# Expert router on DVE: tokens and routing weights transposed in 32 x 32 blocks, DMAs that exchange the blocks, logits in plain fp32 on four column quarters

## What is computed

```python
x = x + layernorm(attention(layernorm(x)))      # 16 heads of 16 channels, softmax over 1024 keys
x = x + layernorm(experts(layernorm(x)))

def experts(x):                                 # xf: 8192 tokens x 256
    logits = l2norm(xf) @ l2norm(gate_w).T      # 16 experts
    scores = sigmoid(logits)
    topk_scores, topk_idx = top_k(scores, 8)
    combine = one_hot(topk_idx) * (topk_scores / sum(topk_scores))      # summed over k: tokens x 16
    y = (silu(xf @ w_gate[e]) * (xf @ w_up[e])) @ w_down[e]             # for every expert e, hidden size 128
    routed = sum over e of y[e] * combine[:, e]
    shared = (silu(xf @ sw_gate) * (xf @ sw_up)) @ sw_down
    return routed + shared
```

## Time and profile before

| what | us |
|---|---|
| median of 3 runs (range) | 2789.33 (2788.68 to 2798.21) |
| profiled execution, its own time | 2794.4 |
| its span, first to last instruction | 2792.5 |
| TensorE matmul busy | 2700.3 (97%) |
| DVE busy | 2203.7 (79%) |
| ACT busy | 1628.2 (58%) |
| POOL busy | 1040.4 (37%) |

### The profile page before, as it was taken

The page is one execution under the profiler, slowest core; times in us unless marked ns, Lnnn a source line. Parts: engine busy times, 40 slices in busy tenths (PEclk is TensorE's granted clock), DMA queues, the critical chain, the costliest instruction groups (busy, mean ns, idle before and its releaser), DMA issues.

```text
span 2792.5 us, 49038 instructions
## 1 busy us (share of the span) xinstructions
PE 2700.3 (97%) x17634; PEld 1775.7 (64%) x17634; DVE 2203.7 (79%) x4585; ACT 1628.2 (58%) x3159; POOL 1040.4 (37%) x1057
## 2 busy tenths in 40 slices
PE   5999999999999999999998999999999999999997
PEld 3445445454454444544543488888888888888886
DVE  5799999989989999999899566666666666666654
ACT  1588888878878788788788733333333333333332
POOL 4042563644635636545358353111111111111112
PEclk8899999999999999999999999999999999999999
DMA  5102333122122222330232323222222222223222
GB/s 119 27 28 58 70 76 72 57 62 66 43 66 66 69 65 64 73 66 28 66 93 76 94 71 101 80 71 75 84 84 82 75 76 84 80 69 84 80 73 54
DMA packets 126595, 197.39 MB, mean 71 GB/s; under 512 B 12288, under 2 KB 74768, under 8 KB 124304
## 3 DMA queue, kind: packets, MB, share of 16 engines
q1 hardware_dynamic: 126352, 194.25, 26.8%
HBM read 108.74 MB, written 17.30 MB: 45 GB/s over the span
## 4 chain that ended last, share of the span: by engine, by line
PE 80%; DVE 13%; ACT 3%; issue 2%; POOL 1%; DMA 0%; POOLq 0%; SPq 0%; ACTq 0%; DVEq 0%
PE o_bank L597 14%; PE y_bank L775 14%; PE g_bank L761 13%; PE u_bank L761 13%; PE st_bank L568 10%; DVE score_max L1164 10%; PE sm_bank L587 8%; PE job_bank L587 2%; ACT probs L1056 2%; PE sm_bank L693 2%; PE job_bank L693 1%; DVE qk_parts L1187 1%; PE job_bank L716 1%; PE job_bank L729 0%; DVE row_max L1171 0%
## 5 line engine op out<-in xcount | busy, mean ns | idle before, releaser
L1056 ACT ACTIVATE probs<-st_bank 128x512 f32<-128x512 f32 x2023 | 1079.2, 603 | 268.9 <-PE st_bank L568 258.6
L1164 DVE TENSOR_REDUCE score_max<-sm_bank 128x1 f32<-128x512 f32 x1601 | 1023.3, 681 | 69.5 <-PE sm_bank L587 63.6
L568 PE MATMUL st_bank<-qk_stack 64*128 64x512 f32 x2023 | 743.4, 427 | 7.1 <-ACT probs L1056 6.9
L587 PE MATMUL sm_bank<-qk_stack 64*128 64x512 f32 x1601 | 655.8, 461 | 27.8 <-DVE score_max L1164 22.1
L597 PE MATMUL o_bank<-probs,v_quad 128*32 128x512 f32 x4096 | 552.7, 612 | 0.7 <-ACT probs L1056 0.7
L568 PEld LDWEIGHTS st_bank<-qk_stack 64*128 64x128 f32 x2023 | 350.2, 186 | 274.7 <-ACT probs L1056 232.6
L587 PEld LDWEIGHTS sm_bank<-qk_stack 64*128 64x128 f32 x1601 | 288.7, 189 | 296.8 <-DVE score_max L1164 268.3
L1312 DVE TENSOR_TENSOR h<-gate_act,u_bank 128x512 f32<-128x512 f32 x256 | 176.2, 688 | 310.9 <-ACT gate_act L1010 310.7
L1010 ACT ACTIVATE gate_act<-g_bank 128x512 f32<-128x512 f32 x272 | 162.4, 597 | 416.0 <-PE u_bank L761 415.9
L1021 ACT ACTIVATE h_hi<-h 128x512 fp32r<-128x512 f32 x272 | 172.1, 633 | 327.8 <-DVE h L1315 290.2
L1595 POOL TENSOR_SCALAR f_x_in<-f_x_in,f_mv,f_rstd 128x256 f32<-128x256 f32 x64 | 90.3, 1422 | 617.2 <-DVE f_rstd L1226 617.2
(11 more groups left out here) (248 smaller groups left out, 4854.6 us busy)
## 6 DMA issues: line engine op xcount, KB each, us to landing
cb<-comb_dram SPq DMA_DIRECT2D x256, 256.0 KB, 3.5
qk_stack<-qk_parts SPq DMA_DIRECT2D x180, 256.0 KB, 5.5
x_in<-in_x SPq DMA_DIRECT2D x8, 1024.0 KB, 5.5
o_part<-o_sb SPq DMA_DIRECT2D x64, 128.0 KB, 2.7
sum_part<-o_sb SPq DMA_DIRECT2D x64, 128.0 KB, 2.8
x_res<-in_x SPq DMA_DIRECT2D x16, 512.0 KB, 3.9
x<-x_res SPq DMA_DIRECT2D x16, 512.0 KB, 4.1
f_x_in<-x SPq DMA_DIRECT2D x16, 512.0 KB, 3.9
```

Of the source, the lines that this page charges most:

```text
L568: mm(bank_of(tile)[:, :], k_stack[q][p][rows, kc * CH:(kc + 1) * CH], q_stack[q][p][rows, f * HALF:(f + 1) * HALF], start=True, stop=True) ...
L587: mm(shared_bank[bank][:, :], q_stack[q][p][rows, tok:tok + CH], k_stack[q][p][rows, half * HALF:(half + 1) * HALF], start=True, stop=True ...
L1056: nc.scalar.activation(probs[kc % 2][:, HEAD_AT[j], :], bank_of(4 * U + j)[:, :], ACT.Exp).then_inc(exp_done, 1)
L1164: v.reduce_max(score_max[f][:, HC * (2 * p + e) + c, half:half + 1], shared_bank[max_bank[n]][:, :], AX_X).then_inc(smax_read, 1)
```

## The change

The transposes of the router leave TensorE. For the tokens, SP issues 16 DMAs (`swap`), from SBUF to SBUF, which exchange the 32 x 32 blocks between the partition quarters and the channel quarters of each 128 x 128 tile, in pieces of 32 floats; DVE then transposes within the blocks (`turn_x`, twice 128 x 512), back into `fx_in`, which now holds the transposed tokens in plain fp32. `xt_hi` and `xt_lo` read them there. The logits take them as moving operand in plain fp32: two steps k of four products, each with the gate weights (32 columns, of which 16 repeat the others) as stationary operand, 128 token columns, and its own quarter of the output partitions. DVE turns the logits (`turn_logits`) and the routing weights (`turn_comb`) too, and four DMAs store the latter. The order of the pieces changes: the layer norm's statistics begin in the group before (e = 14 to 16), the swap comes at e = 7 (`SWAP_AT`), `turn_x` at 7, `xt_hi` and `xt_lo` at 8 and 9, and the load of the tokens of g + 2 at e = 13. In group 0's router the swap stands ahead of the weight loads of experts 12 to 16.

```diff
+        def transposed_x(k):
+
+            return fx_in[:, :, :].rearrange("p (k c) d -> p k (c d)", k=KD)[:, k, :]
+
+
+        comb_flat = comb_dram.rearrange("e t -> (e t)")
+
+        def comb_row(g, e):
+            return comb_flat[(g * EXPERTS + e) * GROUP:(g * EXPERTS + e + 1) * GROUP]
...
             def store_comb(g):
-                wait_apart(sp, E["cbT_read"], g + 1, f_passed["sp"])
-                sp.dma_start(comb_dram[:, bass.ds(g * GROUP, GROUP)], combT[:, :]).then_inc(E["comb_stored"], 16)
+                wait_apart(sp, E["comb_turned"], g + 1, f_passed["sp"])
+                rows = comb_flat[g * EXPERTS * GROUP:(g + 1) * EXPERTS * GROUP].rearrange(
+                    "(p c a j) -> a p c j", p=BLOCK, c=HALVES, a=BLOCKS)
+                for a in range(BLOCKS):
+                    sp.dma_start(rows[a], combT[BLOCK * a:BLOCK * (a + 1), :].rearrange("p (c j) -> p c j", c=HALVES)
+                                 ).then_inc(E["comb_stored"], 16)
+
+            def swap(g):
+
+                wait_apart(sp, E["f_x_normed"], GC * (g + 1), f_passed["sp"])
+                if g == 0:
+                    sp.wait_ge(E["gT_ready"], KD)
+                    sp.wait_ge(E["sq_ready"], GC)
+                else:
+                    wait_apart(sp, E["xT_ready"], KD * g, f_passed["sp"])
+                rows = fx_in[:, :, :].rearrange("p c (k f) -> p (c k) f", k=KD)
+                for b in range(BLOCKS):
+                    for a in range(BLOCKS):
+                        sp.dma_start(swapped[BLOCK * a:BLOCK * (a + 1), :, BLOCK * b:BLOCK * (b + 1)],
+                                     rows[BLOCK * b:BLOCK * (b + 1), :, BLOCK * a:BLOCK * (a + 1)]
+                                     ).then_inc(E["x_swapped"], 16)
 
             def load_cb(g, e):
                 if e == 0:
-                    wait_apart(sp, E["comb_stored"], 16 * (g + 1), f_passed["sp"])
+                    wait_apart(sp, E["comb_stored"], 16 * BLOCKS * (g + 1), f_passed["sp"])
                     if g == 0:
                         sp.wait_ge(st_ready, 4 * UNITS * BATCHES)
                 n = EXPERTS * g + e
                 if not (isinstance(n, int) and n < 4):
                     wait_apart(sp, E["h_done"], n - 3, f_passed["sp"])
                 sp.dma_start(cb[e % 4][:, :],
-                             comb_dram[e, bass.ds(g * GROUP, GROUP)].partition_broadcast(128)).then_inc(cb_loaded[e % 4], 16)
...
                 gather(b, 5)
                 load_shift(b, 7)
                 if last:
+                    swap(0)
                     for e in range(EARLY, ALL_E):
                         load_w(e)
-                    sp.wait_ge(E["xT_ready"], KD)
-                    sp.wait_ge(E["sq_ready"], GC)
+                gather(b, 6)
+                if last:
+                    sp.wait_ge(E["xT_read"], KD)
+                    sp.wait_ge(E["lg_ready"], 1)
                     f_load_x(1)
...
+                    if e == SWAP_AT and not last:
+                        swap(g + 1)
+                    if e == 13 and g + 2 < GROUPS:
+                        wait_apart(sp, E["xT_read"], KD * (g + 2), f_passed["sp"])
+                        wait_apart(sp, E["lg_ready"], g + 2, f_passed["sp"])
+                        f_load_x(g + 2)
...
             def lg(g, par):
                 take_bank("LG", g, 0)
-                pe.wait_ge(E["xT_read"], KD * (g + 1))
+                pe.wait_ge(E["xT_ready"], KD * (g + 1))
                 if isinstance(g, int) and g == 0:
                     pe.wait_ge(E["gT_read"], KD)
...
+                for k in range(KD):
+                    tokens = transposed_x(k).rearrange("p (c a j) -> p a c j", a=BLOCKS, j=BLOCK)
+                    for a in range(BLOCKS):
+                        last = mm(job_bank[BLOCK * a:BLOCK * (a + 1), 0:CH], gT[:, k, :], tokens[:, a, :, :],
+                                  start=(k == 0), stop=(k == KD - 1), skip_group_check=True)
                 last.then_inc(E["lg_ready"], 1)
...
-                    if not last and e in (4, 5):
-                        xt(g + 1, 1 - par, e - 4)
                     if not last and e == 7:
                         lg(g + 1, 1 - par)
-                    if not last and e == 12:
-                        cbt(g + 1)
...
-                a_(fxT[par][0][:, k, :], job_bank[:, :], ACT.Identity).then_inc(E["xT_hi_ready"], 1)
+                a_(fxT[par][0][:, k, :], transposed_x(k), ACT.Identity).then_inc(E["xT_hi_ready"], 1)
...
+                to = x_sq[:, :] if g == 0 else job_bank[:, D:2 * D]
+                a_(to, fx_in[:, c, :], ACT.Square, accum_out=n2[:, c:c + 1]).then_inc(E["sq_ready"], 1)
...
+            def turn_x(g, k):
+                dve.wait_ge(E["x_swapped"], 16 * BLOCKS * BLOCKS * (g + 1))
+                dve.wait_ge(E["sq_ready"], GC * (g + 1))
+                blocks = swapped[:, :, :].rearrange("p (c k) f -> p k c f", k=KD)[:, k, :, :]
+                v.transpose(transposed_x(k).rearrange("p (c f) -> p c f", c=GC), blocks).then_inc(E["xT_ready"], 1)
+
             def xt_lo(g, par, k):
                 dve.wait_ge(E["xT_hi_ready"], KD * g + k + 1)
-                v.tensor_tensor(fxT[par][1][:, k, :], job_bank[:, :], fxT[par][0][:, k, :].bitcast(F32),
+                v.tensor_tensor(fxT[par][1][:, k, :], transposed_x(k), fxT[par][0][:, k, :].bitcast(F32),
                                 ALU.subtract).then_inc(E["xT_read"], 1)
 
-            def sum_logits(g):
-                dve.wait_ge(E["lg_small_read"], g + 1)
+            def turn_logits(g):
+                dve.wait_ge(E["lg_ready"], g + 1)
+                if g > 0:
+                    dve.wait_ge(E["route_chain"], ROUTE * g)
+                v.transpose(lg_turns[:, :, :].rearrange("p c e -> p (c e)"), job_bank[:, 0:CH]).then_inc(E["lg_turned"], 1)
+
+            def scale_logits(g):
+                dve.wait_ge(E["norm_chain"], 12 * (g + 1))
+                dve.wait_ge(E["lg_turned"], g + 1)
                 if g > 0:
                     dve.wait_ge(E["tanh_ready"], g)
-                v.tensor_tensor(logits[:, :, :], lg4(0), lg_small[:, :, :], ALU.add).then_inc(E["lg_summed"], 1)
-
-            def scale_logits(g):
-                dve.wait_ge(E["norm_chain"], 12 * (g + 1))
-                dve.wait_ge(E["lg_summed"], g + 1)
-                v.tensor_tensor(logits[:, :, :], logits[:, :, :], rnorm[:, :, :].to_broadcast([128, GC, EXPERTS]),
+                v.tensor_tensor(logits[:, :, :], lg_turns[:, :, 0:EXPERTS], rnorm[:, :, :].to_broadcast([128, GC, EXPERTS]),
                                 ALU.mult).then_inc(E["lg_read"], 1)
...
-            def cbt_copy(g):
-                dve.wait_ge(E["cbT_ready"], g + 1)
+            def turn_comb(g):
+
+                dve.wait_ge(E["route_chain"], ROUTE * (g + 1))
                 if not (isinstance(g, int) and g == 0):
-                    dve.wait_ge(E["comb_stored"], 16 * g)
-                v.tensor_copy(combT[:, :], job_bank[0:EXPERTS, :]).then_inc(E["cbT_read"], 1)
+                    dve.wait_ge(E["comb_stored"], 16 * BLOCKS * g)
+                v.transpose(combT[:, :], comb[:, :, :].rearrange("p (i c) e -> p c e i", i=HALVES)
+                            ).then_inc(E["comb_turned"], 1)
...
-                if u in (52, 54):
-                    xt_lo(0, 0, (u - 52) // 2)
+                if u in (53, 54):
+                    turn_x(0, u - 53)
+                if u in (55, 56):
+                    xt_lo(0, 0, u - 55)
                 if u == 56:
-                    sum_logits(0)
+                    turn_logits(0)
                     scale_logits(0)
...
+                    turn_comb(0)
+                if u in (61, 62):
+                    ln_stats(1, False, (2 * (u - 61), 2 * (u - 61) + 1))
+                if u == 63:
+                    for n in range(6):
+                        ln_rstd(1, n)
...
-                        if e in (0, 1):
-                            ln_stats(g + 1, False, (2 * e, 2 * e + 1))
-                        if e in (2, 3):
+                        if e == 0:
+                            for n in range(6, 12):
+                                ln_rstd(g + 1, n)
+                        if e == 7:
+                            turn_x(g + 1, 0)
+                            turn_x(g + 1, 1)
+                        if e in (8, 9):
+                            xt_lo(g + 1, 1 - par, e - 8)
+                        if e in (8, 9):
                             for n in range(6):
-                                ln_rstd(g + 1, 6 * (e - 2) + n)
-                        if e in (6, 7):
-                            xt_lo(g + 1, 1 - par, e - 6)
-                        if e in (9, 10):
-                            for n in range(6):
-                                norm_step(g + 1, 6 * (e - 9) + n)
-                        if e == 9:
-                            sum_logits(g + 1)
+                                norm_step(g + 1, 6 * (e - 8) + n)
```

(50 more changed lines are left out.)

42 lines of the change are left out of this document (11 added, 31 removed).

## The result

The changed kernel took 2760.36 us in the median (2759.19 to 2761.96, 4 runs), the kernel before 2792.74 in the same job: ratio 0.9882, 95% interval 0.9863 to 0.9901. The forecast was 2751, range 2742 to 2785.

What follows compares the result with a forecast made beforehand. TensorE's matmul work was taken to bound the kernel. Fifteen groups gain 36.9 us, the first router loses 1, group 0 gains 2: -38 us, so a span near 2754.5 and a median of 2751, range 2742 to 2785.

Steps and rivals of the forecast that it cites:

- TensorE alone sets a group: Expert stage: nothing but matmul work sets a group's length, 74.17 us from one router's logits to the next.
- The logits: Router in each group: eight plain fp32 products take 0.65 us, bounds 0.5 to 1.76; gain 2.46 us a group.
- Rival B: Logits: column quarters do not overlap or short products pay a start, 1.76 us in place of 0.65; 2768, chance 0.13.
- The swap is hidden: Expert 7 of each group: the swap is over 11.1 us after it began, far inside 21.3, so costs nothing.
- the 34 ns taken: Swap's DMA: price of a 128-byte packet, from the weight loads' stretch; 256 on each engine take 8.7 us.
- The cover of 21.3 us: Steady groups: time from the swap's issue until TensorE feels its lateness; it ends at 74 ns a packet.
- The doubling below 512 B: Swap's packets: if small transfers cost double, 68 ns each, the swap takes 19.8 us and the sum stays.
- The first router: Attention part: late swap(0) against TensorE work saved; 1 us lost, bounds 1 gained to 4 lost.
- up to 3 us of wait on ACT: First router: ACT's xt_hi waits from about 1563 for the turned tokens at 1566.2.
- the 1563 of the forecast: First router: time in us when unit 54's exponentials on ACT are over and xt_hi could begin.
- Against it stand the 3.1 us of TensorE: First router: TensorE work that goes there too, set against ACT's wait of up to 3 us.
- Group 0: First expert group: earlier statistics remove ACT's 3.5 us wait for normalised tokens; 2 us gained, bounds 0 to 3.5.

Runs made afterwards that it cites:

- e9: Changed kernel with eight extra TensorE transposes of 128 x 128, read by nobody, ahead of the logits; 2778.20 us.
- e7: Kernel before with only the routing weights turned by DVE and stored in four DMAs, TensorE's block of weight transposes and the copy gone; 2788.87 us.
- e8: Changed kernel with each DVE turn of the tokens done twice from group 1 on; 2763.56 us.
- e5: Changed kernel with all eight logits products written to output partitions 0 to 31 instead of four quarters; 2787.80 us.
- e2: Changed kernel with SWAP_AT = 9 instead of 7, the swap issued later in the group; 2761.99 us.
- e3: Changed kernel with SWAP_AT = 11 instead of 7, the swap issued later still; 2908.20 us.
- e6: Changed kernel with POOL's residual add of 128 x 1024 cut in four of 128 x 256; 2768.08 us.
- e10: The changed kernel once more, unaltered, as partner on the same chip; 2761.32 us, ratio to before 0.9894.
- e1: Changed kernel with swap(0) ahead of the gather and shift load in the last batch instead of behind them; 2757.58 us, ratio to before 0.9865.
- e11: Changed kernel with swap(0) ahead of the gather, run again beside the changed kernel on one chip; 2759.73 us, ratio to before 0.9885.
- e4: Kernel before with only the schedule of the layer norm's statistics taken from the change, a group earlier; 2791.16 us.

## Why the prediction was right, and where it was off

**TensorE alone sets a group: shown.** e9 and e7 price work on TensorE at its full length, e8 prices work on DVE at nothing.

**The logits: mechanism right, term too small.** I took 0.65 between 0.5 and 1.76; they cost 0.77, of which 0.57 are the products. The 0.20 behind them, a longer first projection, I had counted for the old logits (0.10) and not apart for the new. This makes 2.33 in place of 2.46 a group. Rival B, no overlap, is out: e5 shows its period.

**The swap is hidden: right, by other numbers.** SP's timeline and the chain of one group, and a stretch of the first swap, in which the queue had nothing else to move:

```profile
2112.51 10.41 SPq L457 DMA_DIRECT2D swapped<-f_x_in  x16
...
2134.90 0.57 PE job_bank L754 x16
...
1562.00:1564.00 2.00, 0.00 (x0) 0.00 (x0) 0.00 (x0) 0.00 (x0) 0.00 (x0) 1.00 0.31 51
```

A DMA is issued every 0.65 us, not 0.495, and lands 1.9 us later: 10.4 + 1.9 = 12.3 us against 11.1. The packets cost less than the 34 ns taken: 51 GB/s for 2 us are about 800 packets of 128 B, and 0.31 x 16 x 2 = 9.9 engine-us for them are some 12 ns each (over all 69632 such packets in the trace the mean is 12.1). The 256 on an engine thus need 3.1 us, not 8.7: it is the issue on SP that sets the length of the swap. The queue's busy share as a whole rose less, from 26.8% to 28.1%, as the 2 KB packets (most are the cb loads') took 103 ns on average in place of 113. The cover of 21.3 us held to a few tenths (e2, e3), in part by luck: it was worked out to h_lo(7), but TensorE first needs the turned tokens for the logits, which leaves 2134.90 - 2112.51 - 2 x 0.69 = 21.0, almost the same. What the Trainium skill says in "DMA: Bandwidth & Descriptors" (Why small descriptors are slow), that SBUF to SBUF is spared, fits these 12 ns, for packets of 512 B took 27.7; but the 4096 packets of 128 B that went to DRAM in e7 took 11.9 too. The doubling below 512 B that was worked out from its Specifications is not to be seen in any of them.

**The first router: mis-sized, and inside its bounds by luck.** I put the loss at 1 us (1 gained to 4 lost); it was 3.8 in the changed kernel's profile, the least of eight executions with this attention stage (the others 4.1 to 7.3). The step that failed is "up to 3 us of wait on ACT": it was 7.87. Two things made it longer, and one was not given back:

- The issue of the swap took 11.0 us and not 7.9. Where ACT came when the forecast has it (15.1 to 16.6 us behind the mark in e2, e3, e5, e6, e8 and e9; the 1563 of the forecast is 15.4), mainly this made a wait of 5.1 to 5.9 (the swap also began up to 1.3 us later than forecast).
- In the changed kernel and e10 ACT came 4 us sooner, at 1558.8, because the clock stayed at full speed there: a pv that takes 1.86 us in the trace of before (1549.42) takes 1.00 in the changed kernel (1549.07). I had read ACT's time from the trace of before, in which the clock was at half behind the mark, and "at full speed" from the slices of the earlier trace rows, where 10 us at half in 70 still give a 9. The transposes that are gone are not the cause: e1 and e11 are without them too, and ACT came at 14.8 and 15.1.
- "Against it stand the 3.1 us of TensorE" was too much. With no wait at all e1 and e11 gain 0.6 to 1.8 on before, e4 and e7.

The 10 us behind the mark in the trace of before (third number from the end: the clock):

```profile
1548.00:1558.00 10.00, 9.74 (x35) 2.98 (x38) 3.70 (x12) 6.14 (x13) 2.50 (x2) 0.50 0.23 72
```

That the swap landed where I had put it (1565.5 forecast, 1565.9 seen) was luck: it began 1.4 us sooner than forecast and took longer. e1 and e11 show that the order on SP's queue was the cause of the wait.

**Group 0: 2 us forecast, 1.6 by the statistics (e4).** The first of the 15 groups gave 2.0 and not 2.33, as the block at e = 12 lies behind its logits and counts in the next stretch.

**Sum.** -38 forecast, -32.8 in the profiles: 1.9 from the logits (15 x 0.13), 2.8 from the first router, 0.4 from the statistics. The median is 9.4 above the forecast, 4.2 of it from outside the sum: the forecast median was put 3.5 below its span, since the profiled execution of before was 5 above its median, and here the median lies 0.7 above the span.

## What to carry to other kernels

Where one engine's own work is the whole chain, price an edit by that engine's instructions alone, and for all others work out the time between when something is ready and when that engine needs it: here the groups came out to a few tenths of a microsecond. An arrival that is read from one trace holds at the clock of that trace: look at the granted clock in the stretch itself, in windows of a few microseconds, as the digits of the page hide 10 us at half. Take the price of issuing a DMA from a row of the same form where there is one, and otherwise give it a bound. A load that something waits for belongs ahead of what nothing waits for yet on the issuing queue, as in e1.

## What the hardware showed unexpectedly

A small DVE instruction with two operands in SBUF can last as long as a POOL instruction beside it (2435 ns with POOL's 2.40 us add, 773 with four shorter ones, 225 in the kernel before). The Trainium skill has it in "SBUF — State Buffer" (Who interferes with whom): DVE with two SBUF inputs contends with a POOL instruction that reads SBUF, for a pair of ports that one holds for its whole instruction while the other is blocked; these durations agree. Pieces of 128 bytes between SBUF partitions cost about 12 ns of a DMA engine each, while SP's issue of such a DMA takes 0.65 us against 0.5 for the weight loads. A turn of 128 x 512 in blocks takes 686 ns on DVE, as long as the other float32 passes of this size here (675 to 693). After 7.6 us of TensorE standing still the clock was granted at half, which added about a third to the price of the wait. And the same attention stage, at the same place, ran at full clock in two executions and at half for some 10 us in six others.
